# Rotary tables scaled once per layer, and the norms' rounding and rest moved to ScalarE and GpSimd, in a stacked attention and state-space kernel

## Chip, core and metric

The kernel runs on one core of a Trainium2 chip. Its engines work side by side, each through its own queue in order: TensorE (PE, with its weight loads PEld), VectorE (DVE), ScalarE (ACT), GpSimd (POOL), and SyncE (SP), which issues the DMAs. They wait for each other with semaphores. The metric is the device time of one launch in microseconds (us); lower is better. The median of three runs of the kernel before is 3386.6 us (3373.16 to 3394.69).

## What is computed

The input is x, 8 sequences of 256 tokens with 128 features. The whole is a half step of a six-layer stack, a state-space block, and the same half step again:

```
x = x + 0.5 * ffn_ref(layernorm(x), Wqkv, q_scale, k_scale, Wo, ln_g, ln_b, W1, b1, W2, b2)
x = x + attn_ref(layernorm(x), ...)          # selective scan, 16 states
x = x + 0.5 * ffn_ref(layernorm(x), the same weights)
```

One of the six layers of ffn_ref has attention in windows of 32 with 16 heads of 64, and then a gated feed-forward block. What matters here is how queries and keys are made:

```
q = l2norm(q) * qs                     # qs, ksc: one scale per feature and layer
k = l2norm(k) * ksc
q = q * cos * scale + rotate_half(q) * sin * scale
k = k * cos * inv + rotate_half(k) * sin * inv
sim = einsum(q, [keys of this window and of the one before]) * 8, masked, softmax
out = (attn @ v) @ Wo
```

## The kernel before

Features lie on the partitions and tokens along the free dimension. Two sequences (512 tokens) make a chunk, four chunks make the batch. A layer on a chunk is an **item**: 24 items for each of the two stacks, 48 in all. Inside an item the 16 heads go by pairs, one pair a **step**, 8 steps to an item. The lists of every engine are written by one plan (`PLAN`, one `Step` object for each step): an item's projections are made in its own 8 steps, and its later stages follow at fixed lags while the next items are projected. Thus the engines' orders are fixed by the plan and by the order of the `if` lines in `tensor_stack`, `vector_stack`, `scalar_stack` and `gpsimd_stack`. Between the two stacks runs the state-space block.

The steps that matter, counted within an item (n is the item whose projections run; m = n - 1 is the item before it):

- In every step PE projects q and k (L656 to L658, three matmuls each, the first q, later k), ACT squares each (L1085), DVE multiplies each by the sine table and the cosine table (`dve_rotate`, L868 and L874), SP moves the sine products 32 partitions over (L587), and POOL adds them (L1259). PE sums the squares by head (L730).
- Step 0: DVE turns the sums of squares of item m from columns to rows (`dve_norms`, L911), bounds them below (L913) and inverts them (L915). Later in that step it sums a group's exponentials (L952) and inverts the sum (L957), then takes the maximum of the next group (L946).
- Step 1: ACT takes square roots of the inverses: eight small ones for the queries (L1112), one for the keys (L1115). `dve_norms_back` on DVE rounds the keys' roots to the short format (L922), subtracts to get the rest (L924) and turns both back (L927). ACT copies the turned rows to `inv_parts` (`act_norms_high`, L1121), at the end of its step. In the same step PE has the first half of an output projection (L668) and the gates of the feed-forward block (L759), and DVE adds that projection to x (L904), rotates k, and turns a group of probabilities (`dve_turn`, L966).
- Step 2: PE spreads the norms over the partitions (`pe_spread`, L738, waits for `inv_parts`) and then makes the first group of scores of item m (`pe_scores`, L719). Before its square of q, ACT writes the mask into the scores' banks (L1137), and PE waits for that too. All that PE has later in its list stands behind these two waits.
- A group of scores passes POOL three times: minus the maximum (L1265), times the queries' norms (L1273), times the inverse sum (L1279).

PE writes its projections, scores, attention values and so on into 7 PSUM banks in turn; a bank is free when DVE or ACT has read it (for a projection: when L874 is done). `norm_t` holds the turned sums and their parts, `inv_norm` the keys' parts turned back, `k_inv` their spread form.

Of the kernel before, what the change touches and what calls it, by code (L numbers as in the profile page):

```python
# [9 lines left out]
F32R = mybir.dt.float32r  # L10
# [354 lines left out]
xs_hi xs_lo proj_q proj_k squared_q squared_k cos_q cos_k sin_q sin_k moved0 moved1 rotated_q rotated_k  # L365
# [13 lines left out]
def macaron_kernel(nc, x_in, consts_in, vec_in, mvec_in, wqkv_in, wo_in, w1_in, w2_in,  # L379
                   mw_in, wb_in, out):  # L380
    ctx = ExitStack()
    with ctx:
# [29 lines left out]
        squares = sb("squares", [P, 4, COLS])  # L412
        sines = sb("sines", [P, 2, 2, COLS])
        partner = sb("partner", [P, 2, 2, COLS])
        inv_norm = sb("inv_norm", [P, COLS])
        norm_t = sb("norm_t", [P, ITEM_WINS, WIN])
        q_scale8 = sb("q_scale8", [P, 2, GROUPS, ITEM_WINS])
        k_inv = sb("k_inv", [P, WIN + COLS])
        inv_parts = sb("inv_parts", [P, COLS], F32R)
# [24 lines left out]
        mw = sb("mw", [P, 4, P])  # L444
        wbc = sb("wbc", [P, P])
# [85 lines left out]
        def sync_stack(e, w, k):  # L531
# [10 lines left out]
            if k == 0:  # L542
                e.dma_start(mw[:, :, :], mw_in.rearrange("m d n -> d m n")).then_inc(S["m_loaded"], 16)
                e.dma_start(wbc[:, :], wb_in).then_inc(S["m_loaded"], 16)
                e.dma_start(mvec[:, :], mvec_in).then_inc(S["m_loaded"], 16)
            else:
                store_bases(e, w, k)
                meet(w)
            for st in PLAN:
# [8 lines left out]
                if st.load:  # L558
                    layer, p = st.load

                    w.wait_ge(S["wqkv_lo"], (k * DEPTH + layer) * PAIRS + p - 2 if p >= 3 else (k * DEPTH + layer) * PAIRS)
                    e.dma_start(wqkv_raw[:, p % 3, :], wqkv_in[layer][:, p, :]).then_inc(S[f"raw{p % 3}_loaded"], 16)
            for c in range(CHUNKS):
# [275 lines left out]
        def dve_var(e, w, key):  # L839
# [3 lines left out]
            w.wait_ge(S["k_norms_turned"], turned["norms"])  # L843
            e.transpose(var_t.rearrange("p w k -> p (w k)"), general_of(("var", key))[:, :]).then_inc(S["ln_var_kept"], 1)
# [14 lines left out]

        def dve_rotate(e, w, k, n, p, which):  # L860
            m, side, layer = k * ITEMS + n, SIDE[which], n // CHUNKS
            i = m * PAIRS + p
            g, scale = by_seq(general_of(("proj", k, n, p, which))[:, :]), vcol(layer, V_QS + which)
            w.wait_ge(S["vec_loaded"], 16)
# [3 lines left out]
            e.scalar_tensor_tensor(out=by_seq(sines[:, i % 2, which, :]), in0=g, scalar=scale, in1=both(tables[:, 2 * which + 1, :]),  # L868
                                   op0=ALU.mult, op1=ALU.mult).then_inc(S[f"sin_{side}"], 1)

            held = n * PAIRS + p - RING
            if held >= 0:
                w.wait_ge(S["scored"], (k * ITEMS + held // PAIRS) * GROUPS + held % PAIRS // 2 + 1)
            e.scalar_tensor_tensor(out=by_seq(qk_ring[which][:, slot_of(n, p), :]), in0=g, scalar=scale,  # L874
                                   in1=both(tables[:, 2 * which, :]), op0=ALU.mult, op1=ALU.mult).then_inc(S[f"cos_{side}"], 1)
# [30 lines left out]
        def dve_norms(e, w, k, n):  # L906
            m = k * ITEMS + n
            w.wait_ge(S["squares_summed"], (m + 1) * (PAIRS // 2))
            w.wait_ge(S["k_norms_turned"], m)
            w.wait_ge(S["ln_rstd_turned"], turned["roots"])  # L910
# [6 lines left out]
        def dve_norms_back(e, w, k, n):  # L917

            m = k * ITEMS + n
            w.wait_ge(S["k_root"], m + 1)  # L920
            root, low, high = (norm_t[:, :, i * NORM_ROWS:(i + 1) * NORM_ROWS] for i in range(3))
            e.tensor_copy(high.bitcast(F32R), root).then_inc(S["norms_high"], 1)  # L922
            w.wait_ge(S["norms_high"], m + 1)
            e.tensor_tensor(low, root, high, ALU.subtract).then_inc(S["norms_low"], 1)  # L924
            w.wait_ge(S["norms_low"], m + 1)
            w.wait_ge(S["inv_parts"], m)
            e.transpose(inv_norm[:, :], norm_t.rearrange("p w h -> p (w h)")).then_inc(S["k_norms_turned"], 1)  # L927
# [60 lines left out]
        def vector_stack(e, w, k):  # L988
# [4 lines left out]
            for st in PLAN:  # L993
# [11 lines left out]
                if st.norms_back is not None:  # L1005
                    dve_norms_back(e, w, k, st.norms_back)
# [14 lines left out]
                if st.turn:  # L1021
                    dve_turn(e, w, k, *st.turn)
                if st.norms is not None:
# [702 lines left out]
```

## Time and profile before

The profiled execution has a span of 3373.6 us from the first to the last instruction; the median of the three timed runs, 3386.6 us, is 13.0 us above that.

| what | value |
|---|---|
| median (range) of 3 runs | 3386.6 us (3373.16 to 3394.69) |
| span of the profiled execution | 3373.6 us |
| mean granted TensorE clock | 0.938 of full |
| DVE busy | 2981.4 us, 88% |
| PE busy | 2905.4 us, 86% |
| POOL busy | 2425.2 us, 72% |
| ACT busy | 2061.4 us, 61% |
| DMA moved | 250.85 MB, mean 74 GB/s |

How to read it: the two stacks fill most of the span, and in them DVE and PE are both close to nine tenths busy in nearly every slice of the page. Busy shares are averages over the whole; which engine is waited for changes from step to step, so the rows below are mostly from inside one item. A row "x16" merges consecutive instructions of one kind. "Idle before" is the time an engine stood still ahead of an instruction, and the name behind the arrow is what ended it. "issue" stands for idle time for which the profile shows no releaser.

### The profile page before, as it was taken

To read this page: it belongs to the slowest core of one execution; us is meant where nothing else is said; L and a number is where in the kernel's file an instruction comes from. 1 tells how busy PE (TensorE), PEld (TensorE's weight loads), DVE (VectorE), ACT (ScalarE), POOL (GpSimd) and SP (SyncE) were. 2 spreads that over 40 slices of the span, in tenths; PEclk is the share of its full clock that TensorE was granted. 3 is DMA by queue.
4 is the path that set the end of the run, shared out by engine and by line. 5 is a ranking of instruction groups with operands and counts; after the bars stand their busy time and mean duration, and the time that the engine had idled before them with its cause. 6 is when DMAs were issued, how large, how long until landed. Compare 5 with 4: busy or idle time off the path is not lost. (4 is left out here: it accounts for less than half of the span.)

```text
span 3373.6 us, 132100 instructions
## 1 busy us (share of the span) xinstructions
PE 2905.4 (86%) x57914; PEld 1846.3 (55%) x57914; DVE 2981.4 (88%) x4200; ACT 2061.4 (61%) x3820; POOL 2425.2 (72%) x1679
## 2 busy tenths in 40 slices
PE   5788889989989899987767788998999988999987
PEld 3455555655655555653323455565566655565653
DVE  6789899999999899896898878989999989899994
ACT  3466566666666665664764456666666666566663
POOL 3678777787787687774454667778788787787773
PEclk8899999999999999998887889999999999999998
DMA  5233332333333333320001333333343333333330
GB/s 140 65 83 73 82 91 68 89 90 72 86 92 71 84 85 71 83 72 28 7 7 44 80 72 79 75 87 86 75 97 76 90 84 72 81 94 71 86 76 14
DMA packets 114726, 250.85 MB, mean 74 GB/s; under 512 B 27244, under 2 KB 60648, under 8 KB 114152
## 3 DMA queue, kind: packets, MB, share of 16 engines
q1 hardware_dynamic: 114152, 242.40, 30.3%
q8 instruction: 457, 7.49, 1.0%
q14 instruction: 117, 0.96, 0.1%
HBM read 37.82 MB, written 3.15 MB: 12 GB/s over the span
## 5 line engine op out<-in xcount | busy, mean ns | idle before, releaser
L1085 ACT ACTIVATE squares<-general 128x512 f32<-128x512 f32 x768 | 453.9, 597 | 720.8 <-PE general L658 712.2
L1279 POOL TENSOR_TENSOR probs<-probs,row_sum 128x1024 f32<-128x1024 f32 x192 | 365.3, 1903 | 426.3 <-DVE row_sum L957 425.5
L1259 POOL TENSOR_TENSOR q_ring<-q_ring,partner 128x512 f32<-128x512 f32 x384 | 491.1, 1279 | 216.6 <-DMA partner<-sines 216.3
L868 DVE SCALAR_TENSOR_TENSOR sines<-general,vec,consts 128x512 f32<-128x512 f32 x768 | 560.7, 730 | 68.4 <-ACT squares L1085 65.5
L1259 POOL TENSOR_TENSOR k_ring<-k_ring,partner 128x512 f32<-128x512 f32 x384 | 490.8, 1278 | 0.0
L692 PE MATMUL general<-probs_t,v_buf 32*64 32x64 f32 x24576 | 339.4, 236 | 158.3 <-issue 87.0
L656 PE MATMUL general<-xs_hi,wqkv_lo 128*128 128x512 f32 x768 | 457.3, 595 | 15.8 <-DVE xs_lo L897 7.6
L692 PEld LDWEIGHTS general<-probs_t,v_buf 32*64 32x64 f32 x24576 | 305.6, 135 | 248.8 <-issue 241.7
L1273 POOL TENSOR_TENSOR probs<-probs,q_scale 128x1024 f32<-128x1024 f32 x192 | 365.3, 1903 | 15.1
L668 PE MATMUL general<-att,wo 128*128 128x512 f32 x768 | 370.4, 627 | 6.5 <-ACT att L1155 5.2
L719 PE MATMUL general<-k_ring,q_ring 64*32 64x64 f32 (+1 forms) x24576 | 294.2, 224 | 88.4 <-issue 53.5
L1265 POOL TENSOR_TENSOR probs<-probs,row_max 128x1024 f32<-128x1024 f32 x192 | 366.5, 1909 | 0.1
L719 PEld LDWEIGHTS general<-k_ring,q_ring 64*32 64x32 f32 x24576 | 260.0, 106 | 122.6 <-issue 103.4
L657 PE MATMUL general<-xs_lo,wqkv_hi 128*128 128x512 f32 x768 | 315.7, 411 | 2.7 <-issue 2.7
L658 PE MATMUL general<-xs_hi,wqkv_hi 128*128 128x512 f32 x768 | 314.5, 409 | 0.7 <-issue 0.5
L656 PEld LDWEIGHTS general<-xs_hi,wqkv_lo 128*128 128x128 f32 x768 | 153.7, 200 | 264.6 <-issue 233.4
L1155 ACT ACTIVATE att<-general 128x256 f32<-128x256 f32 x768 | 231.3, 388 | 97.0 <-PE general L692 95.6
L891 DVE STREAM_TRANSPOSE v_buf<-general 128x512 f32<-128x512 f32 x384 | 265.3, 691 | 27.1 <-PE general L751 27.0
L874 DVE SCALAR_TENSOR_TENSOR k_ring<-general,vec,consts 128x512 f32<-128x512 f32 x384 | 285.1, 742 | 0.0
L874 DVE SCALAR_TENSOR_TENSOR q_ring<-general,vec,consts 128x512 f32<-128x512 f32 x384 | 284.6, 741 | 0.0
L730 PE MATMUL sums<-squares,consts 128*32 128x512 f32 x1536 | 248.4, 612 | 40.4 <-ACT squares L1085 36.1
L952 DVE TENSOR_REDUCE row_sum<-probs 128x16 f32<-128x1024 f32 x192 | 230.6, 1201 | 41.2 <-ACT probs L1162 41.0
(232 smaller groups left out, 6348.2 us busy)
## 6 DMA issues: line engine op xcount, KB each, us to landing
partner<-sines SPq DMA_DIRECT2D x1536, 128.0 KB, 2.3
wqkv_raw<-in_wqkv SPq DMA_DIRECT2D x80, 208.0 KB, 2.7
wo<-in_wo SPq DMA_DIRECT2D x12, 512.0 KB, 5.1
w<-in_w SPq DMA_DIRECT2D x12, 341.0 KB, 3.2
base_dram<-x SPq DMA_DIRECT2D x8, 256.0 KB, 2.4
att<-in_wqkv SPq DMA_DIRECT2D x2, 1024.0 KB, 6.1
sines<-base_dram SPq DMA_DIRECT2D x8, 256.0 KB, 4.0
w<-in_w SPq DMA_DIRECT2D x12, 128.0 KB
```

What stands on the lines that cost most here:

```text
L656: e.matmul(g[:, :], wqkv_lo[:, p, cut], xs_hi[:, r, :], start=True, stop=False)
L657: e.matmul(g[:, :], wqkv_hi[:, p, cut], xs_lo[:, r, :], start=False, stop=False)
L668: done = e.matmul(g[:, :], wo[:, p, :], att[:, p, :], start=(p == OUT_PAIRS[i][0]), stop=(p == OUT_PAIRS[i][-1]))
L692: done = e.matmul(o, lhs, rhs, start=(kb == 0), stop=True, skip_group_check=True)
L719: done = e.matmul(o, qw, kw, start=False, stop=True, skip_group_check=True)
L868: e.scalar_tensor_tensor(out=by_seq(sines[:, i % 2, which, :]), in0=g, scalar=scale, in1=both(tables[:, 2 * which + 1, :]), op0=ALU.mult, ...
L874: e.scalar_tensor_tensor(out=by_seq(qk_ring[which][:, slot_of(n, p), :]), in0=g, scalar=scale, in1=both(tables[:, 2 * which, :]), op0=ALU. ...
L1085: e.activation(squares[:, (2 * p + which) % 4, :], general_of(("proj", k, n, p, which))[:, :], ACT.Square).then_inc(S[f"squared_{side}"], 1)
L1259: e.tensor_tensor(y, y, partner[:, i % 2, which, :], ALU.add).then_inc(S[f"rotated_{side}"], 1)
L1265: e.tensor_tensor(y, y, spread_keys(row_max[:, i % 2, :]), ALU.subtract).then_inc(S["max_off"], 1)
L1273: e.tensor_tensor(y, y, spread_keys(q_scale8[:, n % 2, group, :]), ALU.mult).then_inc(S["q_norms_off"], 1)
L1279: e.tensor_tensor(y, y, spread_keys(row_sum[:, i % 2, :]), ALU.mult).then_inc(S["probs_done"], 1)
```

## The change

Three edits in the stacks, and two in where tiles lie.

1. Ahead of the first pair of each layer DVE multiplies the four rotary tables by the layer's q and k scales into `layer_tables` (`dve_tables`, two instructions a layer: 24 in all). The rotations then are plain products of projection and table (TENSOR_TENSOR) where they had the scale as a third operand (SCALAR_TENSOR_TENSOR).
2. ACT takes the keys' root twice, once written in the short format (the rounded part) and once in full, both ahead of the queries' eight roots. POOL takes the rest by a subtraction (`pool_norms_low`), behind the second of its passes over the scores. DVE keeps only the turn back, which now stands behind `dve_turn` in its list.
3. The turn back writes into `k_inv` (its first 512 columns past the ones), so `inv_norm` is no tile of its own, and waits are added for the changed readers of `norm_t`.
4. The state-space block's weights lie in `wqkv_raw` and are loaded behind the first stack's partner moves instead of at the start.

```diff
+        layer_tables = sb("layer_tables", [P, 4, SEQ])
-        inv_norm = sb("inv_norm", [P, COLS])
+        inv_norm = k_inv[:, WIN:]
...
-        mw = sb("mw", [P, 4, P])
-        wbc = sb("wbc", [P, P])
+        raw_words = wqkv_raw.rearrange("p i c -> p (i c)")
+        mw = raw_words[:, 0:4 * P].rearrange("p (m n) -> p m n", m=4)
+        wbc = raw_words[:, 4 * P:5 * P]
...
+            if k == 0:
+                w.wait_ge(S["wqkv_lo"], DEPTH * PAIRS)
+                e.dma_start(mw, mw_in.rearrange("m d n -> d m n")).then_inc(S["m_loaded"], 16)
+                e.dma_start(wbc, wb_in).then_inc(S["m_loaded"], 16)
+                e.dma_start(mvec[:, :], mvec_in).then_inc(S["m_loaded"], 16)
             for c in range(CHUNKS):
                 w.wait_ge(S[f"base{c}_stored"], 16 * (k + 1))
...
+        def dve_tables(e, w, k, layer, which):
+
+            w.wait_ge(S["vec_loaded"], 16)
+            w.wait_ge(S[f"cos_{SIDE[which]}"], (k * ITEMS + layer * CHUNKS) * PAIRS)
+            cut = slice(2 * which, 2 * which + 2)
+            e.tensor_scalar(layer_tables[:, cut, :], tables[:, cut, :], vcol(layer, V_QS + which), None, ALU.mult)\
+                .then_inc(S["tables_scaled"], 1)
+
         def dve_rotate(e, w, k, n, p, which):
...
-            e.scalar_tensor_tensor(out=by_seq(sines[:, i % 2, which, :]), in0=g, scalar=scale, in1=both(tables[:, 2 * which + 1, :]),
-                                   op0=ALU.mult, op1=ALU.mult).then_inc(S[f"sin_{side}"], 1)
+            e.tensor_tensor(by_seq(sines[:, i % 2, which, :]), g, both(layer_tables[:, 2 * which + 1, :]), ALU.mult).then_inc(S[f"sin_{side}"], 1)
...
-            e.scalar_tensor_tensor(out=by_seq(qk_ring[which][:, slot_of(n, p), :]), in0=g, scalar=scale,
-                                   in1=both(tables[:, 2 * which, :]), op0=ALU.mult, op1=ALU.mult).then_inc(S[f"cos_{side}"], 1)
+            e.tensor_tensor(by_seq(qk_ring[which][:, slot_of(n, p), :]), g, both(layer_tables[:, 2 * which, :]), ALU.mult).then_inc(S[f"cos_{side}"], 1)
...
         def dve_norms_back(e, w, k, n):
 
             m = k * ITEMS + n
-            w.wait_ge(S["k_root"], m + 1)
-            root, low, high = (norm_t[:, :, i * NORM_ROWS:(i + 1) * NORM_ROWS] for i in range(3))
-            e.tensor_copy(high.bitcast(F32R), root).then_inc(S["norms_high"], 1)
-            w.wait_ge(S["norms_high"], m + 1)
-            e.tensor_tensor(low, root, high, ALU.subtract).then_inc(S["norms_low"], 1)
             w.wait_ge(S["norms_low"], m + 1)
-            w.wait_ge(S["inv_parts"], m)
-            e.transpose(inv_norm[:, :], norm_t.rearrange("p w h -> p (w h)")).then_inc(S["k_norms_turned"], 1)
+            w.wait_ge(S["k_norms_off"], 2 * m * GROUPS)
+            e.transpose(inv_norm, norm_t.rearrange("p w h -> p (w h)")).then_inc(S["k_norms_turned"], 1)
...
-                if st.norms_back is not None:
-                    dve_norms_back(e, w, k, st.norms_back)
                 if st.first_split is not None:
...
                 if st.turn:
                     dve_turn(e, w, k, *st.turn)
+                if st.norms_back is not None:
+                    dve_norms_back(e, w, k, st.norms_back)
...
+            inverse, low, high, root = (norm_t[:, :, i * NORM_ROWS:(i + 1) * NORM_ROWS] for i in range(4))
+            e.activation(high.bitcast(F32R), inverse, ACT.Sqrt).then_inc(S["norms_high"], 1)
+            e.activation(root, inverse, ACT.Sqrt).then_inc(S["k_root"], 1)
...
-            w.wait_ge(S["q_scaled"], (m + 1) * 8)
-            e.activation(norm_t[:, :, 0:NORM_ROWS], norm_t[:, :, 0:NORM_ROWS], ACT.Sqrt).then_inc(S["k_root"], 1)
...
+        def pool_norms_low(e, w, k, n):
+            m = k * ITEMS + n
+            low, high, root = (norm_t[:, :, i * NORM_ROWS:(i + 1) * NORM_ROWS] for i in range(1, 4))
+            w.wait_ge(S["norms_high"], m + 1)
+            w.wait_ge(S["k_root"], m + 1)
+            e.tensor_tensor(low, root, high, ALU.subtract).then_inc(S["norms_low"], 1)
...
                 if st.off:
                     pool_scores(e, w, k, *st.off)
+                if st.norms_back is not None:
+                    pool_norms_low(e, w, k, st.norms_back)
```

VectorE from the end of step 0 through step 1 and into step 2 of an item, before. The row of L957 is the inverse sum of step 0; L922 to L927 are `dve_norms_back`, L904 is the addition to x, L966 `dve_turn`.

```order
L957 RECIPROCAL row_sum<-row_sum 128x16
L946 TENSOR_REDUCE row_max<-probs 128x16
L868 SCALAR_TENSOR_TENSOR sines<-general1,vec,consts 128x512
L874 SCALAR_TENSOR_TENSOR q_ring<-general1,vec,consts 128x512
L922 CAST norm_t<-norm_t 128x16x8
L924 TENSOR_TENSOR norm_t<-norm_t 128x16x8
L927 STREAM_TRANSPOSE inv_norm<-norm_t 128x512
L904 TENSOR_TENSOR x<-x,general2 128x512
L868 SCALAR_TENSOR_TENSOR sines<-general6,vec,consts 128x512
L874 SCALAR_TENSOR_TENSOR k_ring<-general6,vec,consts 128x512
L966 STREAM_TRANSPOSE probs_t<-probs 128x1024
L891 STREAM_TRANSPOSE v_buf<-general0 128x16x32
```

The same place on VectorE in the changed kernel (its line numbers are a few higher; L935 is the turn back).

```order
L965 RECIPROCAL row_sum<-row_sum 128x16
L954 TENSOR_REDUCE row_max<-probs 128x16
L882 TENSOR_TENSOR sines<-general1,layer_tables 128x512
L887 TENSOR_TENSOR q_ring<-general1,layer_tables 128x512
L916 TENSOR_TENSOR x<-x,general2 128x512
L882 TENSOR_TENSOR sines<-general6,layer_tables 128x512
L887 TENSOR_TENSOR k_ring<-general6,layer_tables 128x512
L974 STREAM_TRANSPOSE probs_t<-probs 128x1024
L935 STREAM_TRANSPOSE k_inv<-norm_t 128x512
L903 STREAM_TRANSPOSE v_buf<-general0 128x16x32
```

Two instructions have left the list, and the turn back has moved from ahead of the addition to x to behind the rotation of k and the turn of the probabilities.

GpSimd from step 0 into step 2 of an item in the changed kernel. L1295 is the product with the inverse sum, L1281 and L1289 are the passes with the maximum and the queries' norms, L1268 the rotary additions.

```order
L1295 TENSOR_TENSOR probs<-probs,row_sum 128x1024
L1268 TENSOR_TENSOR k_ring<-k_ring,partner 128x512
L1281 TENSOR_TENSOR probs<-probs,row_max 128x1024
L1289 TENSOR_TENSOR probs<-probs,q_scale8 128x1024
L1275 TENSOR_TENSOR norm_t<-norm_t 128x16x8
L1268 TENSOR_TENSOR q_ring<-q_ring,partner 128x512
L1268 TENSOR_TENSOR k_ring<-k_ring,partner 128x512
```

The subtraction (L1275) stands behind four passes that follow the inverse sum of step 0; before the change this list had the other six rows only.

## Rows read from the trace of the kernel before

**Rows 1.** Windows: us, busy time (instructions) by engine, PEclk, DMA share, GB/s.

```profile
202.00:1499.00 1297.00, 1171.57 (x25115) 764.36 (x25122) 1192.00 (x1697) 829.69 (x1565) 1003.06 (x690) 0.96 0.35 81
590.52:617.51 26.99, 26.50 (x601) 17.57 (x600) 26.18 (x38) 15.13 (x29) 18.94 (x14) 1.00 0.35 80
618.73:640.33 21.60, 17.19 (x527) 13.04 (x513) 21.09 (x33) 13.30 (x24) 18.05 (x14) 0.94 0.48 113
```

**Rows 2.** Waits of PE, 202 to 1499 us: us in total, times, longest.

```profile
PE general L692 <- issue: 33.8, 38, 2.8
PE general L719 <- issue: 29.2, 14, 3.3
PE general L692 <- DVE q_ring L874: 23.4, 16, 2.6
PE general L719 <- ACT general L1137: 14.8, 33, 0.5
```

**Rows 3.** Timeline of item n = 9: start us, us, engine, line, instruction.

```profile
582.38 0.21 DVE L957 RECIPROCAL row_sum<-row_sum 128x16 f32<-128x16 f32 x1
...
587.84 0.71 DVE L927 STREAM_TRANSPOSE inv_norm<-norm_t 128x512 f32<-128x512 f32 x1
...
589.05 0.73 DVE L868 SCALAR_TENSOR_TENSOR sines<-general,vec,consts 128x512 f32<-128x512 f32 x1
...
590.36 1.23 DVE L966 STREAM_TRANSPOSE probs_t<-probs 128x1024 f32<-128x1024 f32 x1
591.52 0.67 DVE L891 STREAM_TRANSPOSE v_buf<-general 128x512 f32<-128x512 f32 x1
...
587.78 0.59 ACT L1085 ACTIVATE squares<-general 128x512 f32<-128x512 f32 x1
588.59 0.63 ACT L1121 ACTIVATE inv_parts<-inv_norm 128x512 fp32r<-128x512 f32 x1 [0.22 <-DVE inv_norm L927]
...
590.52 1.52 PE L719 MATMUL general<-k_ring,q_ring 64*32 64x32 f32 x128
```

**Rows 4.** Timeline of item n = 11, the same places and GpSimd.

```profile
702.87 0.21 DVE L957 RECIPROCAL row_sum<-row_sum 128x16 f32<-128x16 f32 x1
...
709.10 0.63 ACT L1121 ACTIVATE inv_parts<-inv_norm 128x512 fp32r<-128x512 f32 x1 [1.52 <-DVE inv_norm L927]
...
708.25 1.90 POOL L1273 TENSOR_TENSOR probs<-probs,q_scale 128x1024 f32<-128x1024 f32 x1
...
710.88 1.48 PE L719 MATMUL general<-k_ring,q_ring 64*32 64x32 f32 x126 [0.53 <-ACT general L1137]
```

**Rows 5.** Waits in the whole span at the spread of the norms.

```profile
PE general L738 <- ACT inv_parts L1121: 10.8, 13, 2.1
...
PEld general L738 <- ACT inv_parts L1121: 10.7, 4, 2.9
```

**Rows 6.** Groups, whole span: count, busy us, mean ns, idle before.

```profile
L868 DVE SCALAR_TENSOR_TENSOR sines<-general,vec,consts 128x512 f32<-128x512 f32 x768 | 560.7, 730 | 68.4 <-ACT squares L1085 65.5 <-DMA partner<-sines 0.3
L1259 POOL TENSOR_TENSOR q_ring<-q_ring,partner 128x512 f32<-128x512 f32 x384 | 491.1, 1279 | 216.6 <-DMA partner<-sines 216.3
L940 DVE TENSOR_TENSOR probs<-general,k_inv 128x512 f32<-128x512 f32 x384 | 245.7, 682 | 23.1 <-PE general L719 21.7 <-ACT k_inv L1143 1.1
L924 DVE TENSOR_TENSOR norm_t<-norm_t 128x128 f32<-128x128 f32 x48 | 89.4, 1862 | 1.7
L922 DVE CAST norm_t<-norm_t 128x128 fp32r<-128x128 f32 x48 | 42.9, 894 | 22.7 <-ACT norm_t L1115 22.7
```

**Rows 7.** Single lines: duration ns min/median/max, first and last start.

```profile
L924 DVE TENSOR_TENSOR norm_t<-norm_t x48: 1234/1892/2011, 76.7 to 3280.5; 128x128 f32<-128x128 f32 x48
L1516 DVE TENSOR_SCALAR squares<-squares x2: 400/410/420, 1588.2 to 1751.6; 128x512 f32<-128x512 f32 x2
```

**Rows 8.** Timeline of VectorE, two kinds of product back to back.

```profile
606.15 0.73 DVE L874 SCALAR_TENSOR_TENSOR q_ring<-general,vec,consts 128x512 f32<-128x512 f32 x1
606.80 1.27 DVE L940 TENSOR_TENSOR probs<-general,k_inv 128x512 f32<-128x512 f32 x2
607.99 0.74 DVE L980 SCALAR_TENSOR_TENSOR x<-general,vec,x 128x512 f32<-128x512 f32 x1
```

**Rows 9.** Windows of PE alone: us, busy time (instructions), PEclk, DMA share, GB/s.

```profile
634.90:637.80 2.90, 0.58 (x54) 1.00 0.22 51
637.80:641.20 3.40, 3.40 (x26) 0.50 0.53 121
```

More of the change, by code:

```diff
@@ L364 @@
 shifted raw0_loaded raw1_loaded raw2_loaded first_loaded wqkv_hi wqkv_lo wo_loaded w1_loaded w2_loaded
-xs_hi xs_lo proj_q proj_k squared_q squared_k cos_q cos_k sin_q sin_k moved0 moved1 rotated_q rotated_k
+xs_hi xs_lo tables_scaled proj_q proj_k squared_q squared_k cos_q cos_k sin_q sin_k moved0 moved1 rotated_q rotated_k
 squares_summed sums_kept sums_turned sums_inverted q_scaled k_root norms_high norms_low k_norms_turned inv_parts
@@ L541, in sync_stack @@
             load_w2(e, w, k, 0)
[L542 to L546, printed above, removed]
+            if k:
                 store_bases(e, w, k)
@@ L843, in dve_var @@
             w.wait_ge(S["k_norms_turned"], turned["norms"])
+            w.wait_ge(S["q_scaled"], turned["norms"] * 8)
             e.transpose(var_t.rearrange("p w k -> p (w k)"), general_of(("var", key))[:, :]).then_inc(S["ln_var_kept"], 1)
@@ L862, in dve_rotate @@
             i = m * PAIRS + p
-            g, scale = by_seq(general_of(("proj", k, n, p, which))[:, :]), vcol(layer, V_QS + which)
-            w.wait_ge(S["vec_loaded"], 16)
+            g = by_seq(general_of(("proj", k, n, p, which))[:, :])
+            if p == 0 and n % CHUNKS == 0:
+                dve_tables(e, w, k, layer, which)
+            w.wait_ge(S["tables_scaled"], 2 * (k * DEPTH + layer) + which + 1)
             w.wait_ge(S[f"squared_{side}"], i + 1)
             w.wait_ge(S[f"moved{i % 2}"], i // 2 * 64)
-            e.scalar_tensor_tensor(out=by_seq(sines[:, i % 2, which, :]), in0=g, scalar=scale, in1=both(tables[:, 2 * which + 1, :]),
-                                   op0=ALU.mult, op1=ALU.mult).then_inc(S[f"sin_{side}"], 1)
+            e.tensor_tensor(by_seq(sines[:, i % 2, which, :]), g, both(layer_tables[:, 2 * which + 1, :]), ALU.mult).then_inc(S[f"sin_{side}"], 1)
             held = n * PAIRS + p - RING
@@ L909, in dve_norms @@
             w.wait_ge(S["k_norms_turned"], m)
+            w.wait_ge(S["q_scaled"], m * 8)
             w.wait_ge(S["ln_rstd_turned"], turned["roots"])
@@ L1120, in act_norms_high @@
             w.wait_ge(S["norm_spread"], m * GROUPS)
-            e.activation(inv_parts[:, :], inv_norm[:, :], ACT.Copy).then_inc(S["inv_parts"], 1)
+            e.activation(inv_parts[:, :], inv_norm, ACT.Copy).then_inc(S["inv_parts"], 1)
         def act_gelus(e, w, k, n):
@@ L1387, in tensor_part @@
                     g = pe_bank(w, ("m_bc", c))
-                    e.matmul(g[:, :], wbc[:, :], m_u[c], start=True, stop=True).then_inc(S["m_bc"], 1)
+                    e.matmul(g[:, :], wbc, m_u[c], start=True, stop=True).then_inc(S["m_bc"], 1)
         def pe_added(e, w, at):
```

## The prediction

> **What bounds the kernel now.** I read the page first, then windows over the first stack, then PE's waits, then the timeline of single items.
>
> Take the even part of the first stack, 202 to 1499 us. Two items take 120.5 us (the inverse sums of step 0 at 582.59 and 703.08, [rows 3, 4]), so some 21 items lie in these 1297 us. VectorE is busy 1192 of 1297 us and PE 1172 [rows 1]: neither share says which one to relieve. PE's waits say how much of PE's idle time another engine causes: VectorE's release of banks 23.4 us, the masks 14.8 us, against 63.0 us in which nothing shown released it [rows 2].
>
> Inside an item the limits take turns. Windows of item n = 9 show it. From the first scores (590.52) to the end of the projection of q in step 6 (617.51), PE is busy 26.50 of 26.99 us: this stretch is PE's own work, and if it starts later it ends later. From the rotation of that q (618.73) to the inverse sum in step 0 (640.33), VectorE is busy 21.09 of 21.60 us and PE 17.19: this stretch is VectorE's [rows 1]. What is left of the cycle is the stretch from the inverse sum in step 0 to the first scores in step 2: from 582.59 to 590.52, 7.93 us, in item 9 [rows 3], and from 703.08 to 710.88, 7.80 us, in item 11 [rows 4]. The norms lie in this last stretch, and there the change moves things. A price must be asked of each stretch by itself.
>
> **The norms' path.** Before, VectorE turns the norms back at 587.84 in item 9, ahead of its rotation of k; ScalarE copies them at 588.59, PE starts the scores at 590.52 [rows 3]. In the changed order the turn back stands behind the addition to x, the rotation of k and the turn of the probabilities, and it also waits for GpSimd's subtraction. Two paths lead to it, and the later counts.
>
> *Through the rotation of k.* The k of step 1 is squared at 588.37 (587.78 + 0.59). VectorE is free by then, since it has lost the two instructions of the norms, and rotates at 588.40. Two products at 0.60 each (below) end the rotation at 589.60. The turn of the probabilities takes 1.16 from its start to the next one's (590.36 to 591.52): 590.76. The turn back takes 0.71: 591.47. ScalarE's copy starts 0.03 later, 591.50. Before, this copy started at 588.59 and the scores came 1.93 later, but in item 9 PE was the late one; in item 11, where PE stood waiting for the masks, it is 1.78 (709.10 to 710.88) [rows 3, 4]. So the first scores start at 593.28 where they started at 590.52: 2.76 us later. PE's list is in order, and all behind it shifts.
>
> *Through GpSimd.* In item 11 GpSimd's pass with the queries' norms ends at 710.15 (708.25 + 1.90) [rows 4]. The subtraction follows. The trace shows no 128-element operation on GpSimd; 512 elements with two inputs take 1.279 us [rows 6]. A quarter of that, 0.32, is the bound below and the whole the bound above; I take 0.45, near the quarter, for a fixed part on top. Then 710.60, the turn back and its semaphore 0.75: 711.35, and 1.78 more: 713.13 where the scores started at 710.88: 2.25 us later.
>
> Which case is how frequent? PE or its weight load waits at the spread for the copied norms 13 + 4 = 17 times in 48 [rows 5]. These are the items of the second kind, with PE early; the other 31 are like item 9. So 17 x 2.25 + 31 x 2.76 = 124 us later in all. Its bounds: with GpSimd's 0.32 the first kind falls to 2.12 (122 us in all); with 1.28 it rises to 3.08 and the sum to 138.
>
> What VectorE gets back in this stretch is much on paper. L922 and L924 take 0.894 and 1.862 us and the wait ahead of them 22.7 us in 48 items, 155 us together [rows 6]. But with them gone it would stand at the rotation of k, waiting for PE and ScalarE, and later at the turn back. I price it at nothing; the cover that eats it is the path above. Its worth if that cover were not there is in the first rival. ScalarE's second root lies ahead of its gelus, which wait for PE's gates, and costs nothing unless these are late.
>
> **The rotations.** 1536 of them lose the third operand. Start to start, one with three operands takes 0.65 us (606.15 to 606.80) and a product of PSUM with SBUF takes 0.595 (two in 606.80 to 607.99) [rows 8]. The means, 730 and 682 ns, differ by nearly the same [rows 6]. So 0.055 to 0.06 us each, 92 us of VectorE's time at the most. It is paid out only in VectorE's own stretch, with about 10 of an item's 32: 0.6 us x 46 items = 28 us less. The bounds are nothing and 92.
>
> **The tables.** 24 products of 128x512 from SBUF to SBUF. Such a row takes 0.41 us beside the scan [rows 7]. Beside a busy GpSimd small operations on `norm_t` are stretched: the rounding of 128x128 averages 0.894 us, and the subtraction has a median of 1.892 us and a minimum of 1.234 for a quarter of the elements [rows 6, 7]. I take 0.9 each, 22 us, between 10 (at 0.41) and 45 (at 1.89), in VectorE's own stretch.
>
> The Trainium skill, SBUF — State Buffer, "Who interferes with whom", explains this stretching: a VectorE instruction with two SBUF inputs, or a one-source one in a two-port mode, and a GpSimd instruction that reads SBUF exclude each other for a whole instruction; the trace agrees (1.89 us at the median, the length of GpSimd's pass beside it, 1.90).
>
> **The rest.** GpSimd gains 48 x 0.45 = 22 us of work, in a list that waits 216.3 us for the partner moves [rows 6]: nothing. The block's weights are three DMAs behind the last partner moves of stack one, once; 0 to 4 us, I take 0.
>
> **The sum.** 124 - 28 + 22 = +118 us. On the profiled span that is 3373.6 + 118 = 3491.6; with the 13.0 us by which the median lies above, 3504.6 us. I say **3505**, 3.5% slower. This case alone has a range of 3440 to 3565: below, with 64 us more gained by the rotations (92, not 28) or part of PE's unexplained waits hidden in the new stall; above, with the tables at 45, the GpSimd bound at 138 and some loss of clock.
>
> **The rivals.**
>
> *VectorE's relief decides (faster).* By busy shares VectorE loses 155 + 92 - 22 = 225 us of work. PE could take that up only as far as it waits for others: 23.4 + 14.8 us in 21 items [rows 2], 87 us in 48. Time: 3386.6 - 87 = 3300. For it speaks VectorE's 92% in the stack; against it that item 9 has no idle PE from the scores to step 6 and that the norms now lie behind the k of step 1. It decides where the scores start less than 0.13 us later an item, (28 - 22) / 46, than before. Chance 0.11.
>
> *The new stall swallows the old ones (no change).* PE's waits without a releaser are 63.0 us in 21 items at these two lines [rows 2], 144 us in 48. If two thirds of them come to lie inside the new wait, 118 - 96 = +22: 3409. Against it: they come at L692 and L719, behind the wait and not ahead of it. Chance 0.12.
>
> *The stall also costs clock (slower still).* When PE had stood nearly still, busy 0.58 of 2.90 us, it ran the next 3.40 us at 0.50 of the full clock, the lower of its two levels, 1.2 GHz [rows 9]. A stall of 2.3 to 2.8 us in every item could do so each time, for 1.7 us: 48 x 1.7 = 82, 3587. Against it: a clock of 0.96 over 1297 us [rows 1] is 8% at half, 104 us, some 30 such spells in 21 items that are there already, and would partly be replaced. Chance 0.13.
>
> *GpSimd's subtraction takes as long as VectorE's did.* At 1.89 us in place of 0.45, the first kind of item loses 3.69 and not 2.25: 17 x 1.44 = 24 us more, 3529. Chance 0.04. The Trainium skill's Perfetto Trace Analysis, "Optimizing Scalar/DVE Operations", says that moving work between VectorE and GpSimd "might not help" for the port they share; no row here shows the subtraction on GpSimd.
>
> **How the numbers follow.** My forecast has 0.60, the clock 0.13, GpSimd 0.04, no change 0.12, faster 0.11. About 1% (34 us) is what a measurement of this kernel can tell from no change: faster means under 3353, slower over 3420. Slower 0.77, same 0.12, faster 0.11. The range from 3385 to 3590 leaves out the faster case and little else.
>
> **What would show it.** In the profile of the changed kernel: PE's waits get a new head, L738 (and L719 behind the masks), some 2.3 to 2.8 us in nearly every item; the turn back on VectorE waits for GpSimd only in items with PE early, and VectorE's rotation of k waits for ScalarE's square. From the scores to step 6 PE's busy time stays 26.5 us. VectorE's busy time falls by some 225 us while the span grows. Rotations near 0.68 us, the two-port products near 0.9, GpSimd's subtraction near 0.45. I am wrong if PE hardly waits at L738: then the stretch from inverse sum to scores stayed near 7.9 us, and the relief counts.

## The result

The changed kernel takes 3491.9 us (median of four runs, 3486.9 to 3495.0), the kernel before 3380.0 us over its runs beside and ahead of it (3373.2 to 3394.7). The ratio is 1.0327, with a 95% interval from 1.0287 to 1.0367: 3.3% slower. The prediction was 3505 us, from 3386.6. On the profiled executions the span went from 3373.6 to 3485.1 us, 111.5 us more; the sum had 118.

**The profile after.** First line: the page's busy time by engine. Then windows of the same three kinds of stretch as in [rows 1] (us, busy time by engine, PEclk, DMA share, GB/s): the even part of the first stack; from the first scores to step 6 of one item; from the rotation of q in step 6 to the inverse sum in step 0.

```profile
PE 2934.4 (84%) x57914; PEld 1853.2 (53%) x57914; DVE 2805.9 (81%) x4128; ACT 2064.3 (59%) x3868; POOL 2445.7 (70%) x1727
```

```profile
202.00:1540.00 1338.00, 1179.07 (x24955) 763.21 (x24944) 1110.54 (x1659) 828.12 (x1584) 1008.05 (x710) 0.95 0.34 78
```

```profile
797.92:824.71 26.79, 26.64 (x600) 17.56 (x600) 23.88 (x36) 14.98 (x29) 17.73 (x12) 1.00 0.28 63
825.93:847.05 21.12, 19.25 (x533) 14.19 (x519) 20.68 (x34) 15.37 (x28) 17.49 (x13) 0.92 0.39 90
```

VectorE lost 175.5 us of busy time and the span grew by 111.5. PE's own stretch is what it was (26.64 us busy of 26.79; before 26.50 of 26.99), though VectorE now has room in it (23.88, before 26.18). VectorE's stretch is shorter by half a microsecond (21.12, before 21.60) in this item.

One item could mislead, so here are the means over 42 items of either trace (all but the first two and the last of each stack). From the first scores to the rotation of q in step 6: 30.46 us before, 30.40 after. From there to the inverse sum: 22.08 and 22.28. From the inverse sum to the first scores: 8.84 and 11.26. So the whole loss lies in the third stretch. Inside it the way from the inverse sum to the square of k kept its length (6.39 and 6.17), and the way from that square to the scores grew from 2.45 to 5.09.

The waits of the changed kernel (us in total, times, longest):

```profile
DVE sines L882 <- ACT squares L1093: 292.9, 239, 4.1
...
ACT inv_parts L1130 <- DVE k_inv L935: 155.5, 48, 6.0
...
PE general L741 <- ACT inv_parts L1130: 108.2, 46, 5.8
...
PE general L695 <- issue: 67.2, 70, 2.7
...
PE general L722 <- ACT general L1146: 46.5, 97, 0.8
...
PE general L722 <- issue: 39.0, 24, 2.6
...
PEld general L741 <- ACT inv_parts L1130: 23.0, 4, 6.6
DVE k_inv L935 <- POOL norm_t L1275: 20.6, 19, 4.9
```

And those of the kernel before that answer to them beyond [rows 2, 5]:

```profile
PE general L692 <- issue: 87.0, 91, 2.8
...
PE general L719 <- issue: 53.5, 28, 3.3
...
PE general L719 <- ACT general L1137: 34.7, 70, 1.7
```

PE now waits at the spread (L741) in 46 of 48 items, 108.2 us, where it was 10.8 us in 13 [rows 5]: 97 us more. The masks behind it add 12 (46.5, before 34.7). The weight loads' own rows (4 times in either kernel) are the same stalls seen once more: before, the load stood from 1506.68 to 1509.61 and PE from 1507.55 to 1509.61. They are not added. VectorE's relief went into its own wait: its rotations stood still for ScalarE's squares for 65.5 us before [rows 6], and now for 292.9.

One item of the changed kernel, in order of time (start us, us, engine, line; only what carries the path):

```profile
785.61 0.21 DVE L965 RECIPROCAL row_sum<-row_sum 128x16 f32<-128x16 f32 x1
...
792.44 0.59 ACT L1093 ACTIVATE squares<-general 128x512 f32<-128x512 f32 x1
792.83 0.45 POOL L1275 TENSOR_TENSOR norm_t<-norm_t 128x128 f32<-128x128 f32 x1
...
793.07 0.69 DVE L882 TENSOR_TENSOR sines<-general,layer_tables 128x512 f32<-128x512 f32 x1 [3.86 <-ACT squares L1093]
...
794.27 1.23 DVE L974 STREAM_TRANSPOSE probs_t<-probs 128x1024 f32<-128x1024 f32 x1
...
795.43 0.67 DVE L935 STREAM_TRANSPOSE k_inv<-norm_t 128x512 f32<-128x512 f32 x1
...
796.13 0.63 ACT L1130 ACTIVATE inv_parts<-k_inv 128x512 fp32r<-128x512 f32 x1 [2.66 <-DVE k_inv L935]
...
796.91 0.47 PE L741 MATMUL general<-inv_parts,spread_sel 128*128 128x256 f32 x2 [1.89 <-ACT inv_parts L1130]
...
797.91 1.31 PE L722 MATMUL general<-k_ring,q_ring 64*32 64x32 f32 x117 [0.53 <-ACT general L1146]
```

The k is squared at 793.03, VectorE had waited 3.86 us for it, the turn back starts 2.40 us later, and the scores start 4.88 us after the square; in item 9 of the kernel before it was 2.15 us (588.37 to 590.52, [rows 3]). GpSimd's subtraction was done at 793.28, long ahead: here VectorE's own list is the later way.

In another item GpSimd is the later way:

```profile
590.18 0.21 DVE L965 RECIPROCAL row_sum<-row_sum 128x16 f32<-128x16 f32 x1
...
597.41 0.45 POOL L1275 TENSOR_TENSOR norm_t<-norm_t 128x128 f32<-128x128 f32 x1
...
597.89 0.71 DVE L935 STREAM_TRANSPOSE k_inv<-norm_t 128x512 f32<-128x512 f32 x1 [0.41 <-POOL norm_t L1275]
...
598.64 0.63 ACT L1130 ACTIVATE inv_parts<-k_inv 128x512 fp32r<-128x512 f32 x1 [3.63 <-DVE k_inv L935]
...
600.42 1.29 PE L722 MATMUL general<-k_ring,q_ring 64*32 64x32 f32 x113 [0.53 <-POOL k_ring L1268]
```

From the inverse sum (590.39) to the scores it is 10.03 us; the prediction had 10.05 (703.08 to 713.13) for this kind.

The groups that were priced (count, busy us, mean ns):

```profile
L882 DVE TENSOR_TENSOR sines<-general,layer_tables 128x512 f32<-128x512 f32 x768 | 518.0, 675 | 295.0 <-ACT squares L1093 292.9 <-DMA partner<-sines 0.7
...
L1275 POOL TENSOR_TENSOR norm_t<-norm_t 128x128 f32<-128x128 f32 x48 | 21.8, 455 | 0.5 <-ACT norm_t L1115 0.5
L869 DVE TENSOR_SCALAR layer_tables<-consts,vec 128x512 f32<-128x512 f32 x24 | 17.7, 737 | 0.3 <-DVEq L838 0.3
```

### The profile page after: what moved, and what is told of

It is laid out like the page before. It is cut to its first block and busy times, and to the rows that moved or that the text cites. A ratio compares the mean times of both kernels' runs of the same rounds, so it can differ in the third digit from the quotient of the medians.

```text
span 3485.1 us, 132137 instructions
## 1 busy us (share of the span) xinstructions
PE 2934.4 (84%) x57914; PEld 1853.2 (53%) x57914; DVE 2805.9 (81%) x4128; ACT 2064.3 (59%) x3868; POOL 2445.7 (70%) x1727
## 5 line engine op out<-in xcount | busy, mean ns | idle before, releaser
L1295 POOL TENSOR_TENSOR probs<-probs,row_sum 128x1024 f32<-128x1024 f32 x192 | 365.7, 1905 | 601.4 <-DVE row_sum L965 601.4
L882 DVE TENSOR_TENSOR sines<-general,layer_tables 128x512 f32<-128x512 f32 x768 | 518.0, 675 | 295.0 <-ACT squares L1093 292.9
L1268 POOL TENSOR_TENSOR q_ring<-q_ring,partner 128x512 f32<-128x512 f32 x384 | 491.2, 1279 | 121.1 <-DMA partner<-sines 120.7
L1268 POOL TENSOR_TENSOR k_ring<-k_ring,partner 128x512 f32<-128x512 f32 x384 | 491.6, 1280 | 0.0
L659 PE MATMUL general<-xs_hi,wqkv_lo 128*128 128x512 f32 x768 | 468.7, 610 | 17.1 <-DVE xs_lo L909 7.8
L695 PE MATMUL general<-probs_t,v_buf 32*64 32x64 f32 x24576 | 335.7, 238 | 130.8 <-issue 67.2
L722 PE MATMUL general<-k_ring,q_ring 64*32 64x64 f32 (+1 forms) x24576 | 301.1, 233 | 95.2 <-ACT general L1146 46.5
L1289 POOL TENSOR_TENSOR probs<-probs,q_scale 128x1024 f32<-128x1024 f32 x192 | 365.7, 1904 | 15.1
L671 PE MATMUL general<-att,wo 128*128 128x512 f32 x768 | 361.7, 615 | 7.3 <-ACT att L1164 5.6
L1281 POOL TENSOR_TENSOR probs<-probs,row_max 128x1024 f32<-128x1024 f32 x192 | 366.8, 1911 | 0.6 <-DVE row_max L954 0.6
L948 DVE TENSOR_TENSOR probs<-general,k_inv 128x512 f32<-128x512 f32 x384 | 245.1, 678 | 37.6 <-PE general L722 35.5
L752 PE MATMUL general<-xs_hi,wqkv_lo 128*128 128x256 f32 x768 | 262.4, 342 | 4.3 <-issue 4.3
```

What stands on the lines that cost most here:

```text
L659: e.matmul(g[:, :], wqkv_lo[:, p, cut], xs_hi[:, r, :], start=True, stop=False)
L671: done = e.matmul(g[:, :], wo[:, p, :], att[:, p, :], start=(p == OUT_PAIRS[i][0]), stop=(p == OUT_PAIRS[i][-1]))
L695: done = e.matmul(o, lhs, rhs, start=(kb == 0), stop=True, skip_group_check=True)
L722: done = e.matmul(o, qw, kw, start=False, stop=True, skip_group_check=True)
L882: e.tensor_tensor(by_seq(sines[:, i % 2, which, :]), g, both(layer_tables[:, 2 * which + 1, :]), ALU.mult).then_inc(S[f"sin_{side}"], 1)
L1268: e.tensor_tensor(y, y, partner[:, i % 2, which, :], ALU.add).then_inc(S[f"rotated_{side}"], 1)
```

## The experiments

The theory was that the changed kernel loses in one place, between the inverse sum of step 0 and the first scores of step 2, because the norms come back late, on two ways: behind VectorE's rotation of k and turn of the probabilities, and behind GpSimd's two passes. The rivals were the tables with the tile places and moved loads, GpSimd alone, VectorE's place alone, and a stall that PE can absorb. Every run was timed in three rounds beside the kernel before; kernels are compared by their ratios to it, since its own median was 3377, 3367 or 3370 us beside them.

**The tables without the norms' part.** The changed kernel, with `dve_norms_back` at its old place, and ScalarE and GpSimd as before:

```diff
+            w.wait_ge(S["k_root"], m + 1)
+            root, low, high = (norm_t[:, :, i * NORM_ROWS:(i + 1) * NORM_ROWS] for i in range(3))
+            e.tensor_copy(high.bitcast(F32R), root).then_inc(S["norms_high"], 1)
+            w.wait_ge(S["norms_high"], m + 1)
+            e.tensor_tensor(low, root, high, ALU.subtract).then_inc(S["norms_low"], 1)
             w.wait_ge(S["norms_low"], m + 1)
...
+                if st.norms_back is not None:
+                    dve_norms_back(e, w, k, st.norms_back)
                 if st.first_split is not None:
...
                     dve_turn(e, w, k, *st.turn)
-                if st.norms_back is not None:
-                    dve_norms_back(e, w, k, st.norms_back)
...
-            e.activation(high.bitcast(F32R), inverse, ACT.Sqrt).then_inc(S["norms_high"], 1)
-            e.activation(root, inverse, ACT.Sqrt).then_inc(S["k_root"], 1)
...
+            w.wait_ge(S["q_scaled"], (m + 1) * 8)
+            e.activation(norm_t[:, :, 0:NORM_ROWS], norm_t[:, :, 0:NORM_ROWS], ACT.Sqrt).then_inc(S["k_root"], 1)
...
-                if st.norms_back is not None:
-                    pool_norms_low(e, w, k, st.norms_back)
```

> The changed kernel with the norms put back as they were (root on ScalarE behind the queries' roots, rounding and rest on VectorE, turn back ahead of the rotation of k); the tables, the tile places and the moved loads stay as changed. My theory (the norms' path alone makes the kernel slower): about 28 us less for the rotations and 18 us more for the tables against the kernel before, 3360 to 3385 us; PE hardly waits for inv_parts at the spread. Rival (tables, tile places or moved loads make it slower): 3420 us or more.

Measured: 3361.3 us, ratio 0.9956 (0.9928 to 0.9984), 15 us less than before. PE's wait at the spread is short:

```profile
PE general L741 <- ACT inv_parts L1134: 14.3, 17, 3.7
```

So tables, tile places and moved loads are not the loss; together they are a small gain. What makes it is open: in the profile PE's busy time fell by as much as the time (2905.4 to 2886.0 us, at a mean clock of 0.945 and not 0.938), and VectorE's own stretch did not become shorter on average (22.08 to 22.31 us over the same 42 items).

**The norms' part without the tables.** The changed kernel with the three-operand rotations of before and no call of `dve_tables`; the cosine's product is changed in the same way:

```diff
-            e.tensor_tensor(by_seq(sines[:, i % 2, which, :]), g, both(layer_tables[:, 2 * which + 1, :]), ALU.mult).then_inc(S[f"sin_{side}"], 1)
+            e.scalar_tensor_tensor(out=by_seq(sines[:, i % 2, which, :]), in0=g, scalar=scale, in1=both(tables[:, 2 * which + 1, :]),
+                                   op0=ALU.mult, op1=ALU.mult).then_inc(S[f"sin_{side}"], 1)
```

> The changed kernel without the layer's tables: rotations with three operands as before, the norms' parts and places as changed. My theory (the two edits add up): the tables were worth 16 us where they stood alone, so 10 to 20 us over the changed kernel: 3500 to 3515 us. Rival (the rotations' savings are lost in the new stall): 3480 to 3495 us.

Measured: 3501.2 us, ratio 1.0394 (1.0359 to 1.0429), against the changed kernel's 1.0327. The difference, 0.67% or 23 us, has intervals of 0.4% on both sides and holds the 15 us from above. The two edits add up as far as this can be measured. The theory's range, 3500 to 3515, is met, and the rival's, 3480 to 3495, is missed.

**GpSimd's subtraction first.** VectorE's turn back stays late.

```diff
                 if st.norms_back is not None:
+                    pool_norms_low(e, w, k, st.norms_back)
+                if st.off:
+                    pool_sub(e, w, k, *st.off)
...
                 if st.off:
                     pool_scores(e, w, k, *st.off)
-                if st.norms_back is not None:
-                    pool_norms_low(e, w, k, st.norms_back)
```

> The changed kernel with GpSimd's subtraction ahead of its two passes over the scores; VectorE's turn back stays late. My theory (in most items the way through VectorE's rotation of k and turn of the probabilities is the later one): VectorE's 20.6 us of waits for GpSimd go, the third of the items with PE early gains about 0.65 us each, in all 5 to 20 us against the changed kernel: 3470 to 3487 us. Rival (the late subtraction on GpSimd is the cause): most of the 112 us come back, 3420 us or less.

Measured: 3465.5 us, ratio 1.0251 (1.0215 to 1.0287), 26 us less than the changed kernel, where 5 to 20 were expected.

```profile
PE general L741 <- ACT inv_parts L1130: 89.3, 46, 4.1
...
DVE k_inv L935 <- POOL norm_t L1275: 1.0, 1, 1.0
```

VectorE no longer waits for GpSimd, and PE still waits 46 times. GpSimd alone is not the cause.

**The turn back at its old place.** GpSimd's subtraction stays late.

```diff
+                if st.norms_back is not None:
+                    dve_norms_back(e, w, k, st.norms_back)
                 if st.first_split is not None:
...
                 if st.turn:
                     dve_turn(e, w, k, *st.turn)
-                if st.norms_back is not None:
-                    dve_norms_back(e, w, k, st.norms_back)
```

> The changed kernel with VectorE's turn back at its old place, ahead of the addition to x and the rotation of k; GpSimd's subtraction stays late. My theory: the scores start some 10.05 us after the inverse sum in every item instead of 8.76 before and about 11.4 after; VectorE waits for GpSimd in every item, about 5 us each. About half of the loss stays: 3420 to 3465 us. Rival (only the place on VectorE matters): about 3365 us.

Measured: 3433.8 us, ratio 1.0169 (1.0142 to 1.0196): half of the loss stays.

```profile
DVE k_inv L935 <- POOL norm_t L1275: 243.9, 46, 7.4
...
PE general L741 <- ACT inv_parts L1130: 74.5, 35, 5.1
```

VectorE stands at the turn back 5.3 us an item for GpSimd, and PE behind it. VectorE's place alone is not the cause either.

**Both early.** The two edits above together.

> The changed kernel with both moved: the subtraction ahead of GpSimd's passes over the scores, the turn back at its old place on VectorE. The subtraction can then be done about 3.7 us after the inverse sum, the turn back about 4.5 us after it, before PE wants it. My theory: no stall at the spread, the whole loss goes, and what is left is the small gain: 3335 to 3375 us, a little faster than the kernel before. Rival (the two engines exclude each other, or VectorE's relief counts in full): 3400 us or more, or 3300 us and less.

Measured: 3333.3 us, ratio 0.9865 (0.9832 to 0.9898): the whole loss is gone, and the kernel is 1.35% faster than the one before. It lies just under the range.

```profile
DVE k_inv L935 <- POOL norm_t L1275: 68.1, 47, 3.5
...
PE general L741 <- ACT inv_parts L1130: 8.0, 4, 4.4
```

Either edit leaves a loss of 1.7% or 2.5%, both together turn it: each of the two ways is enough to hold PE. Between this kernel and the changed one lie 4.6%, about 156 us; in the profiled spans it is 146.5 us, of which 100 are PE's wait at the spread and 45 are PE's busy time (2888.9 and 2934.4), at a mean clock of 0.943 and 0.928.

**How much each instruction ahead of the turn back costs.** With the subtraction first, the turn back was moved over one instruction of VectorE at a time. First ahead of the turn of the probabilities:

```diff
+                if st.norms_back is not None:
+                    dve_norms_back(e, w, k, st.norms_back)
                 if st.turn:
                     dve_turn(e, w, k, *st.turn)
-                if st.norms_back is not None:
-                    dve_norms_back(e, w, k, st.norms_back)
```

> GpSimd's subtraction first, and the turn back behind the rotation of k but ahead of the turn of the probabilities (1.16 us start to start). My theory: 48 x 1.16 = 56 us less than with the turn back behind the turn of the probabilities (3465.5 us), so 3400 to 3420 us; PE still waits at the spread, some 1.2 us an item. Rival: within 10 us of 3465.

Then behind the turn of v:

```diff
                 if st.turn:
                     dve_turn(e, w, k, *st.turn)
-                if st.norms_back is not None:
-                    dve_norms_back(e, w, k, st.norms_back)
...
                 if st.v:
                     dve_v(e, w, k, *st.v)
+                if st.norms_back is not None:
+                    dve_norms_back(e, w, k, st.norms_back)
```

> GpSimd's subtraction first, and VectorE's turn back one instruction later than in the changed kernel, behind the turn of v (0.6 us start to start). My theory (what VectorE has ahead of the turn back delays the scores, one for one): 48 x 0.6 = 29 us over the kernel with the subtraction first and the turn back where the change put it (3465.5 us): 3485 to 3505 us. Rival (PE's stall only takes the place of other idle time): no more than 5 us over it.

Measured: 3389.7 us, ratio 1.0063 (1.0036 to 1.0089), and 3494.4 us, ratio 1.0358 (1.0312 to 1.0405). The first lies below the range in microseconds; by the ratios it is 1.9% under the subtraction-first kernel (1.0251), 63 us, for 48 x 1.16 = 56. The second is 1.1% over it, 36 us, for 48 x 0.6 = 29. PE's waits at the spread, in this order:

```profile
PE general L741 <- ACT inv_parts L1130: 40.8, 46, 4.6
```

```profile
PE general L741 <- ACT inv_parts L1130: 116.2, 46, 4.2
```

From 40.8 over 89.3 to 116.2 us: what VectorE has ahead of the turn back reaches PE at nearly its full length. The time moves by more, because of the clock. From the first of these kernels to the one with the subtraction first, PE's wait grows by 48.5 us and the span by 83; PE's busy time grows by 52 (2885.2 to 2937.1), at a mean clock of 0.947 and then 0.926. The second step adds 27 us of wait, 7 of busy time and 34 of span.

**The place alone, in the kernel before.** Its three instructions moved behind `dve_turn`, nothing else:

```diff
-                if st.norms_back is not None:
-                    dve_norms_back(e, w, k, st.norms_back)
                 if st.first_split is not None:
...
                 if st.turn:
                     dve_turn(e, w, k, *st.turn)
+                if st.norms_back is not None:
+                    dve_norms_back(e, w, k, st.norms_back)
```

> The kernel before with one edit: its rounding, subtraction and turn back on VectorE stand behind the turn of the probabilities, as the turn back does in the changed kernel. No tables, nothing on GpSimd. My theory (the place alone does it): in every item rounding and subtraction (1.3 to 2.8 us) come on top of the 2.8 us that the late place costs, so 200 to 265 us more than before: 3580 to 3640 us. Rival (GpSimd's part is needed for the loss): within 1% of the kernel before.

Measured: 3565.4 us, ratio 1.0577 (1.0534 to 1.062), 198 us more, a little under the range.

```profile
L924 DVE TENSOR_TENSOR norm_t<-norm_t 128x128 f32<-128x128 f32 x48 | 43.0, 896 | 1.7
...
L922 DVE CAST norm_t<-norm_t 128x128 fp32r<-128x128 f32 x48 | 24.5, 510 | 0.0
```

Rounding and subtraction take 1.41 us together at this place and not the 2.76 of [rows 6]. With that, 48 x (2.76 + 1.41) = 200 us. That this meets the 198 is in part luck, since PE's busy time, for which the sum has no term, grew by 46 us (2905.4 to 2951.0, clock 0.917) and the waits by less than the sum. It also says what the move to GpSimd was worth inside the changed kernel: with a late turn back, the two instructions on VectorE cost some 1.41 us an item, 68 us; this kernel lies 1.8%, 62 us, over the one with the norms' part alone (1.0394), in which they are gone from VectorE.

**Behind the addition to x.** The subtraction first, and the turn back between the addition (L916) and the rotation of k:

```diff
                 if st.out_first:
                     dve_out(e, w, k, *st.out_first)
+                if st.norms_back is not None:
+                    dve_norms_back(e, w, k, st.norms_back)
                 if st.root is not None:
...
                     dve_turn(e, w, k, *st.turn)
-                if st.norms_back is not None:
-                    dve_norms_back(e, w, k, st.norms_back)
```

> GpSimd's subtraction first, and the turn back behind the addition to x but ahead of the rotation of k. With both early VectorE waits 1.45 us an item for the subtraction; 0.6 us of that would be filled by the addition. My theory: between no change and 0.6 us x 48 = 29 us less than with both early (3333.3 us), 3305 to 3340 us; no loss unless the addition, which waits for PE, delays the turn back past the time at which PE wants it. Rival (the addition's wait for PE holds the turn back): 3345 us or more.

Measured: 3327.8 us, ratio 0.9871 (0.9832 to 0.991). VectorE's wait for the subtraction falls from 68.1 to 28.7 us, and the time does not follow: the ratio is that of both early.

```profile
DVE k_inv L935 <- POOL norm_t L1275: 28.7, 34, 2.5
```

**Both early, without the tables.** The kernel with both early, and the rotations of before as above.

> Without the layer's tables, with the subtraction first on GpSimd and the turn back at its old place on VectorE. My theory: the norms' part alone, well placed, is worth what both early had (44 us) less the tables' 16 us: some 28 us under the kernel before, 3335 to 3360 us. Rival (all of the gain was the tables'): within 5 us of the kernel before.

Measured: 3346.8 us, ratio 0.9943 (0.9912 to 0.9975). The norms' part is worth 0.6% well placed, 19 us, where 28 were expected; with the tables' 0.4% that is 1.0%, and the two together measured 1.35%. The intervals allow the sum.

## Why the prediction was right, step by step

**The three stretches.** The step that decided all was not to price VectorE's relief by its busy share. PE's stretch kept its length with less work on VectorE beside it, and so did VectorE's. This is shown by the means over 42 items above, and by the kernel with tables alone: some 1500 shorter rotations, and 15 us net.

**The norms' path.** Predicted 124 us in 48 items, 2.76 for the kind where VectorE is the later and 2.25 for the kind where GpSimd is; on average 2.58 an item. The stretch grew by 2.42 an item (8.84 to 11.26). VectorE waited for GpSimd in 19 items. The prediction counted 17, by adding PE's 13 waits and the weight load's 4; these 4 are among the 13, and with 13 its sum is 126, nearly the same. The two ways to the scores came out at 4.88 us from the square (4.91 foretold: 588.37 to 593.28) and 10.03 from the inverse sum (10.05). PE's added waits are 97 us at the spread and 12 at the masks, 109 in all. That both ways are at work, and each enough, is shown by the kernels with one and with both moved.

**GpSimd's subtraction.** 0.455 us; 0.45 was chosen between 0.32 and 1.28. The rival in which it takes 1.89 fell.

**The rotations.** The mean of the sine product went from 730 to 675 ns, as foretold; the cosine product's from 742 to 678. In VectorE's own stretch the median item of three in four became 0.33 us shorter, where 0.6 in every item had been the term, and one item in four, the one with a layer's tables, 1.9 us longer. With the tables the term -28 + 22 stands against a stretch that is 0.2 us longer on average, which the scatter of the items does not tell from nothing. The gain of 15 us of the kernel with tables alone is therefore not shown to be this term.

**The tables.** 0.737 us each, 17.7 us, against 0.9 and 22.

**The two rivals that were each partly true.** *The new stall swallows the old ones:* PE's waits without a releaser at the values and the scores fell from 87.0 + 53.5 to 67.2 + 39.0, by 34 us, where that rival needed 96. *The stall also costs clock:* this one came true in most items. In the 6 us behind an item's first scores PE had less than the full clock in 38 of 48 items, before in 9. The same item before and after (us, PE busy, PEclk, DMA share, GB/s):

```profile
651.22:657.22 6.00, 5.35 (x265) 1.00 0.38 84
```

```profile
666.37:672.37 6.00, 6.00 (x261) 0.72 0.02 5
```

Ahead of the second PE had stood 1.88 us at the spread, and ahead of the first it had not stood there. The other kernels order themselves by this stall: 5 items in 48 with both early (0.2 us on average), 13 with the turn back ahead of the turn of the probabilities (0.9), 26 with only the turn back early (1.5), 36 with only the subtraction early (1.9), 42 with the turn back behind the turn of v (2.4); the changed kernel has 2.3. Over the whole span PE did the same work in 29 us more busy time (2905.4 to 2934.4), at a mean clock of 0.928 instead of 0.938. At half the clock for the missing share, that is 502 us at the lower level where it was 418, worth 42 us at the most. The rival had 82. In part it stayed smaller because the clock was higher elsewhere: in the state-space block, between the last scores of the first stack and the first of the second, it was 0.87, before 0.85.

The 29 us of clock and the 34 us of swallowed waits are about equal, and left the sum nearly where it was. That is luck: the sum had neither. A second pair of misses also offsets itself. Against the kernel with both early, whose third stretch is 8.08 us on average, lateness costs about 156 us, clock included, and the sum had 124; but well placed the change gains 44 us, and the sum had 6.

**VectorE's relief.** 225 us were foretold as the fall of its busy time; it is 175.5. Of the 225, 23 were no work but the wait ahead of the rounding [rows 6], so its own rows gave 202. The groups' own sums fall by more than that: 132 us of rounding and subtraction, 92 of rotations, less 18 of tables is 206. The busy time on the page counts overlapping instructions once, and instructions with gaps between them overlap less; what share of the 30 us that explains is left open. No part of the time hangs on it.

## What to carry to other kernels

Cut the period of a pipelined loop into stretches by the engine that has no idle time in each, and price an edit in the stretch where it lies: here about 200 us less work on the busiest engine made the kernel 3.3% slower, because it lay where that engine then waited anyway. When an instruction is moved down an in-order list, add up what stands ahead of it at its new place, including what those wait for, and follow the result to the engine that stops for it; where that is TensorE, add what the clock takes behind the stall. Work that is handed to another engine needs its place in that engine's list chosen too: with the same instructions, subtraction first and turn back early, the kernel is 1.3% faster than before instead.

## What the hardware showed

How long a small VectorE operation on SBUF takes depends on what GpSimd runs beside it. The subtraction of 128x128 took 1.89 to 2.01 us in 44 of 48 items of the kernel before, beside a GpSimd pass over the scores (1.90 us). In the kernel with the late place alone it took 0.29 us in 19 items in which GpSimd ran nothing beside it, and 1.24 us in 27 beside the rotary additions (1.28 us); the rounding took from 0.18 to 1.91 us, with a median of 0.19. Duration in ns, min/median/max:

```profile
L924 DVE TENSOR_TENSOR norm_t<-norm_t x48: 291/1235/2010, 78.5 to 3471.0; 128x128 f32<-128x128 f32 x48
```

On GpSimd the same subtraction takes 0.455 us and is never stretched (0.448 to 0.468 in 48). So such an operation can be cheaper on the slower engine, when GpSimd would otherwise be running beside it. The Trainium skill, GPSIMD Engine Reference, "3.1 Elementwise — side-by-side cycle accounting", has GpSimd 1.96 times slower at an addition of 2048 elements. The traces agree in the order: 0.455 us is 1.6 times the undisturbed 0.29. It is the time blocked by GpSimd, up to 1.7 us, that turns the order round. The scaling of a table, 128x512, took 0.446 to 0.991 us in the changed kernel.
